# State's product in 32x32 tiles, the out product's last third moved by one step, y's squares summed head by head

## The reference

```
retention:  Q, K = xpos(xn W_Q), xpos(xn W_K)      8 heads of 32; K by the inverse scale
            V    = xn W_V
            Y_h  = (Q_h K_h^T * D_h) V_h           D_h[s,t] = gamma_h^(s-t) for s >= t, else 0
            Yn   = (Y - mean) / sqrt(var + 1e-5)   mean and variance over each head's 32 numbers
            out  = (silu(xn W_G) * (Yn * gn_weight + gn_bias)) W_O
feed-forward: xq = fp4(xn), weights in fp4 too     blocks of 16 along the last dimension
            h    = silu(xq Wgate^T) * (xq Wup^T)   704 wide
            out  = fp4(h) Wdown^T
```

## Time and profile before

| | us |
|---|---|
| median of 3 runs | 902.4 (901.42 to 902.75) |
| the profiled execution | 902.86 |
| its span in the trace | 901.1 |
| PE busy | 868.1 (96%) |
| DVE busy | 834.8 (93%) |
| POOL busy | 679.6 (75%) |
| ACT busy | 495.2 (55%) |

### The profile page before, as it was taken

One profiled execution on the slowest core, in us unless ns is written; L12 is line 12 of the kernel. 1 busy time (PEld: TensorE's weight loads), 2 busy tenths in 40 slices (PEclk: granted clock), 3 DMA queues, 4 the chain that ended last, 5 costly groups with the idle time before them and its releaser, 6 DMA issues.

```text
span 901.1 us, 20383 instructions
## 1 busy us (share of the span) xinstructions
PE 868.1 (96%) x7698; PEld 763.9 (85%) x7698; DVE 834.8 (93%) x1883; ACT 495.2 (55%) x1370; POOL 679.6 (75%) x795
## 2 busy tenths in 40 slices
PE   2889999999999999999999999999999999999996
PEld 1768888888888888888888888888888888888885
DVE  7879999999999999999999999999999999999984
ACT  5655555555555555555555555555555555555542
POOL 4767787777778777777877877787787777778774
PEclk9899999999999999999999999999999999999999
DMA  9200110110111011011101101100110110110000
GB/s 339 73 1 19 36 37 19 36 37 22 32 36 36 19 37 36 20 35 36 33 23 36 36 19 37 36 31 25 36 37 19 36 37 24 31 37 12 8 13 18
DMA packets 30049, 33.62 MB, mean 37 GB/s; under 512 B 3328, under 2 KB 28672, under 8 KB 29696
## 3 DMA queue, kind: packets, MB, share of 16 engines
q1 hardware_dynamic: 29808, 32.26, 11.4%
q10 hardware_dynamic: 144, 0.07, 0.0%
HBM read 23.92 MB, written 8.39 MB: 36 GB/s over the span
## 4 chain that ended last, share of the span: by engine, by line
PE 93%; POOL 3%; DVE 2%; ACT 1%; issue 1%; DMA 0%; POOLq 0%; DVEq 0%
PE quad L899 12%; PE quad L901 12%; PE quad L900 12%; PE quad L1080 5%; PE quad L961 4%; PE quad L984 4%; PE bank L901 3%; PE bank L900 3%; PE bank L899 3%; PE bank L1017 3%; PE quad L1087 3%; PE quad L926 3%; PE quad L1064 3%; PE quad L985 2%; PE quad L949 2%; PE quad L953 2%
## 5 line engine op out<-in xcount | busy, mean ns | idle before, releaser
L899 PE MATMUL quad<-w_gu_hi,xqT_hi 128*128 128x512 f32 (+1 forms) x384 | 150.3, 391 | 0.9 <-DVE xqT_lo L592 0.9
L901 PE MATMUL quad<-w_gu_hi,xqT_lo 128*128 128x512 f32 (+1 forms) x384 | 144.4, 376 | 0.0
L900 PE MATMUL quad<-w_gu_lo,xqT_hi 128*128 128x512 f32 (+1 forms) x384 | 143.3, 373 | 0.0
L463 POOL TENSOR_TENSOR rstd<-var_eps,power 128x9 f32<-128x9 f32 x67 | 124.1, 1853 | 5.6
L452 POOL TENSOR_TENSOR x_quot<-xn,x_inv 128x256 f32<-128x256 f32 x64 | 40.4, 632 | 90.9 <-DVE x_inv L640 90.9
L471 POOL TENSOR_TENSOR xT_lo<-xT_in,xT_hi 128x256 fp32r<-128x256 f32 x64 | 47.4, 740 | 61.7 <-ACT xT_hi L789 61.7
L438 POOL TENSOR_TENSOR h_quot<-h,h_inv 128x704 f32<-128x704 f32 x64 | 88.8, 1388 | 6.3 <-DVE h_inv L583 1.3
L721 ACT ACTIVATE xqT_hi<-bank 128x256 fp32r<-128x256 f32 x64 | 24.6, 384 | 121.1 <-PE bank L934 121.1
L448 POOL TENSOR_TENSOR qk<-qk_cos,qk_sin 128x512 f32<-128x512 f32 x64 | 82.8, 1293 | 7.6 <-PE bank L971 0.9
L487 POOL TENSOR_TENSOR gate_gn<-gate,gn 128x512 f32<-128x512 f32 x64 | 83.3, 1301 | 0.2 <-ACT gate L782 0.2
L901 PEld LDWEIGHTS quad<-w_gu_hi,xqT_lo 128*128 128x128 f32 x384 | 72.5, 189 | 11.5
(11 more groups left out here) (178 smaller groups left out, 2953.6 us busy)
## 6 DMA issues: line engine op xcount, KB each, us to landing
x_in<-in_x_dram SPq DMA_DIRECT2D x64, 128.0 KB, 2.1
xT_in<-in_xT_dram SPq DMA_DIRECT2D x64, 128.0 KB, 2.2
out_dram<-y_out SPq DMA_DIRECT2D x64, 128.0 KB, 1.7
sin<-const_sin_dram SPq DMA_DIRECT2D x1, 1792.0 KB, 10.9
raw<-in_w_gu_dram SPq DMA_DIRECT2D x2, 512.0 KB, 6.5
w_qkvg<-in_w_qkvg_dram SPq DMA_DIRECT2D x1, 1024.0 KB, 7.3
cos<-const_cos_dram SPq DMA_DIRECT2D x1, 896.0 KB, 7.0
raw<-in_w_down_dram SPq DMA_DIRECT2D x2, 352.0 KB, 7.7
```

What stands on the lines that cost most here:

```text
L463: pool.tensor_tensor(rstd[:, (t + 3) % RING, 0:1 + H], var_eps[:], power[:], ALU.pow).then_inc(rstd_ready, 1)
L899: pe.matmul(out, hi[:, k], w_hi[:, k], start=start, stop=False)
L900: pe.matmul(out, hi[:, k], w_lo[:, k], start=False, stop=False)
L901: return pe.matmul(out, lo[:, k], w_hi[:, k], start=False, stop=stop)
```

## The change

Three edits, made together. First, the state stays compact: `state` is the 128x64 sum itself, and its product is eight 32x32 matrix products with 128 moving columns, on eight different tiles of the array: for the first four heads rows r and columns r, for the last four rows r+1 and columns r. For this the last four heads of q and k are stored rotated by one (weights, cos and sin tables in the order `ORDER`), `probs` is read rotated (L961), and K^T V is written rotated (L971). ACT's four copies and POOL's clearing of `state` go. The product moves from ahead of x's transposes to between h's transposes and L961. Second, L1087 moves from the end of step i to behind the q and k product of step i+1, and DVE's y_out moves behind the first half of the masking. Third, ACT squares y with eight instructions of 32 columns, each of which also sums its columns into `moments` (`accum_out`); DVE's sum L648 goes, and POOL waits for ACT alone.

```diff
+ORDER = [*range(HG), *(HG + (r - 1) % HG for r in range(HG))]
-        for h in range(H):
+        for h in ORDER:
-        state_sum = sb("state_sum", [P, G * HD])
-        state = sb("state", [P, D])
+        state = sb("state", [P, G * HD])
+        def quarter(r):
+            return slice(r * HD, (r + 1) * HD)
+        def place(g, r):
+            return quarter((r + g) % HG)
 # POOL
-            pool.memset(state[:], 0.0).then_inc(cleared, 1)
-                        pool.wait_ge(y_var, t + 1)
+                        pool.wait_ge(squared, t + 1)
 # DVE: y_out (sum of b_out and x_in, L576) moves behind masked0 and h_inv
-                    dve.wait_ge(squared, t + 1)
-                    dve.tensor_reduce(moments[:, 2:], heads(y_sq[:]), AX_X, ALU.add).then_inc(y_var, 1)
+                    dve.wait_ge(kv_ready, kept_upto(t))
-                        dve.tensor_tensor(state_sum[:], state_sum[:], b_kv[:, 0:G * HD], ALU.add).then_inc(kv_add, 1)
+                        dve.tensor_tensor(state[:], state[:], b_kv[:, 0:G * HD], ALU.add).then_inc(kv_add, 1)
 # ACT
-                    act.activation(y_sq[:], b_y[:, 0:D], ACT.Square, scale=HD ** -0.5).then_inc(squared, 1)
+                    for head in range(H):
+                        dims = slice(head * HD, (head + 1) * HD)
+                        ins = act.activation(y_sq[:, dims], b_y[:, dims], ACT.Square, scale=HD ** -0.5, accum_out=moments[:, 2 + head:3 + head])
+                    ins.then_inc(squared, 1)
-                    act.wait_ge(kv_add, kept_upto(t))
-                    for r in range(HG):
-                        rows = slice(r * HD, (r + 1) * HD)
-                        ins = act.activation(tiles(state[:])[rows, :, rows], heads(state_sum[:])[rows], ACT.Copy)
-                    ins.then_inc(state_copy, 1)
 # PE, behind the q and k product
-                    pe.wait_ge(state_copy, kept_upto(t - 1))
-                    pe.wait_ge(masked1, t + 1)
-                    for g in range(G):
-                        ins = pe.matmul(b_yT[g], state[:, g * P:(g + 1) * P], qT[:, g, :], start=True, stop=False)
-                    ins.then_inc(st_ready, 1)
+                if exists(i - 3):
+                    t = i - 3
+                    for k in range(KD):
+                        ins = pe.matmul(b_out, zT_lo[:, k], w_out_hi[:, k], start=False, stop=k == KD - 1)
+                    ins.then_inc(out_ready, 1)
 # PE, behind the transposes of h
+                if exists(i - 1) and later(i - 1):
+                    t = i - 1
+                    for g in range(G):
+                        for r in range(HG):
+                            rows = place(g, r)
+                            ins = pe.matmul(b_yT[g][quarter(r), :], state[rows, g * HD:(g + 1) * HD], qT[rows, g, :], start=True, stop=False)
+                    ins.then_inc(st_ready, 1)
-                            ins = pe.matmul(b_yT[g][rows, :], val[:, head:head + HD], probs[:, r, g * P:(g + 1) * P],
+                            ins = pe.matmul(b_yT[g][quarter(r), :], val[:, head:head + HD], probs[:, (r + g) % HG, g * P:(g + 1) * P],
-                            ins = pe.matmul(b_kv[rows, g * HD:(g + 1) * HD], qk[:, D + head:D + head + HD], val[:, head:head + HD],
+                            key, head = D + g * P + place(g, r).start, (g * HG + r) * HD
+                            ins = pe.matmul(b_kv[place(g, r), g * HD:(g + 1) * HD], qk[:, key:key + HD], val[:, head:head + HD],
 # PE, at the end of the step
-                if exists(i - 2):
-                    t = i - 2
-                    for k in range(KD):
-                        ins = pe.matmul(b_out, zT_lo[:, k], w_out_hi[:, k], start=False, stop=k == KD - 1)
-                    ins.then_inc(out_ready, 1)
```

More of the change, by code:

```diff
@@ L223, in block_kernel @@
         x_peak = sem("x_peak")
-        summed = sem("summed")
         masked0 = sem("masked0")
         h_inverted = sem("h_inverted")
+        summed = sem("summed")
         rope_sin = sem("rope_sin")
@@ L238, in block_kernel @@
         x_inverted = sem("x_inverted")
-        y_var = sem("y_var")
         h_gridded = sem("h_gridded")
@@ L283, in block_kernel @@
         x_high = sem("x_high")
-        state_copy = sem("state_copy")
         x_normed = sem("x_normed")
         qk_ready = sem("qk_ready")
-        st_ready = sem("st_ready")
+        out_ready = sem("out_ready")
         x_turned = sem("x_turned")
@@ L293, in block_kernel @@
         h1_turned = sem("h1_turned")
+        st_ready = sem("st_ready")
         yT_ready = sem("yT_ready")
@@ L307, in block_kernel @@
         s_ready = sem("s_ready")
-        out_ready = sem("out_ready")
         def exists(t):
@@ L424, in _ @@
             pool.memset(moments[:], 1.0).then_inc(cleared, 1)
-            pool.memset(state[:], 0.0).then_inc(cleared, 1)
-            pool.wait_ge(cleared, 3)
+            pool.wait_ge(cleared, 2)
             def step(i):
@@ L570, in step @@
                     dve.tensor_reduce(x_max[:], blocks(xn[:, t % 2, :]), AX_X, ALU.max, apply_absolute_value=True).then_inc(x_peak, 1)
[L571 to L576, removed]
                 if exists(i - 1):
@@ L583, in step @@
                     dve.tensor_scalar(h_inv[:], h_rec[:], SIX, 1e12, ALU.mult, ALU.min).then_inc(h_inverted, 1)
+                if exists(i - 3):
+                    t = i - 3
+                    dve.wait_ge(out_ready, t + 1)
+                    if t >= 2:
+                        dve.wait_ge(stored, 16 * (t - 1))
+                    dve.tensor_tensor(y_out[:, t % 2, :], b_out, x_in[:, t % SLOTS, :], ALU.add).then_inc(summed, 1)
                 if exists(i):
@@ L617, in step @@
                     if t == 0:
-                        dve.wait_ge(cleared, 3)
+                        dve.wait_ge(cleared, 2)
                     dve.wait_ge(x_stats, t + 1)
@@ L666, in step @@
                     t = i - 1
+                    dve.wait_ge(kv_ready, kept_upto(t))
                     if t % CHUNKS == 0:
-                        dve.tensor_copy(state_sum[:], b_kv[:, 0:G * HD]).then_inc(kv_add, 1)
+                        dve.tensor_copy(state[:], b_kv[:, 0:G * HD]).then_inc(kv_add, 1)
                     else:
-                        dve.tensor_tensor(state_sum[:], state_sum[:], b_kv[:, 0:G * HD], ALU.add).then_inc(kv_add, 1)
+                        dve.tensor_tensor(state[:], state[:], b_kv[:, 0:G * HD], ALU.add).then_inc(kv_add, 1)
                 if exists(i):
@@ L876, in load_functions @@
             def load_functions():
-                act.wait_ge(cleared, 3)
+                act.wait_ge(cleared, 2)
                 act.activation(scratch[:], power[:], ACT.Silu)
@@ L920, in step @@
                         turn_rest(8)
-                if exists(i - 1) and later(i - 1):
-                    t = i - 1
-                    pe.wait_ge(state_copy, kept_upto(t - 1))
-                    pe.wait_ge(masked1, t + 1)
-                    for g in range(G):
-                        ins = pe.matmul(b_yT[g], state[:, g * P:(g + 1) * P], qT[:, g, :], start=True, stop=False)
-                    ins.then_inc(st_ready, 1)
+                if exists(i - 3):
+                    t = i - 3
+                    for k in range(KD):
+                        ins = pe.matmul(b_out, zT_lo[:, k], w_out_hi[:, k], start=False, stop=k == KD - 1)
+                    ins.then_inc(out_ready, 1)
                 if exists(i):
@@ L959, in step @@
                         for r in range(HG):
-                            rows, head = slice(r * HD, (r + 1) * HD), (g * HG + r) * HD
-                            ins = pe.matmul(b_yT[g][rows, :], val[:, head:head + HD], probs[:, r, g * P:(g + 1) * P],
+                            head = (g * HG + r) * HD
+                            ins = pe.matmul(b_yT[g][quarter(r), :], val[:, head:head + HD], probs[:, (r + g) % HG, g * P:(g + 1) * P],
                                             start=t % CHUNKS == 0, stop=True)
@@ L1193, in layouts @@
     heads = lambda w: w.transpose(0, 2, 1).reshape(D, D)
+    w_q, w_k = w_q[ORDER], w_k[ORDER]
     w_gu = [w[c * GW:min((c + 1) * GW, F)] for c in (2, 1, 0) for w in (w_gate, w_up)]
```

5 lines of the change are left out of this document (removed).

## The result

The changed kernel takes 906.44 us (median of 6 runs, 904.88 to 907.48) against 901.91 us (6 runs, 901.34 to 903.11) for the kernel before on the same chip: ratio 1.0044, 95% interval 1.0034 to 1.0054. It is slower by 0.44%; forecast was 902.2, no change. The profiled execution took 906.24 with a span of 904.4, that is 3.4 and 3.3 more than before.

What follows compares the result with a forecast made beforehand. PE was taken as the bound, with z on POOL limiting savings ahead of its transposes. From 902.86 us, -0.7 for the steps and +0.5 for the ends gave 902.7 profiled, 902.2 median; range 896 to 917.

Steps and rivals of the forecast that it cites:

- the size of the state's product in 32x32 tiles: PE, behind z's transposes: sixteen 32x32 instructions, eight tiles at once, taken as 0.33 us per step.
- the extra: PE, between the state's product and L961: 0.09 us more for changing form from 32x32 to 128x32.
- the second weight load: PE, L1087 behind the 32-row scores: 0.11 us per step lost, expected to go once q and k follow the scores.
- the cap: PE ahead of z's transposes: waiting for POOL's z limits the saving to 0.35 of 0.55 us per step.
- Rival D: PE at z's transposes: no wait for z, the full 0.55 us is had, -13.2 us, 889.5; chance 0.05.
- Rival B: PE, state's product: four passes at a time whatever the tiles, 0.44 or 0.57 us, 908.5 or 915.8; chance 0.30.
- Rival A: PE, state's product: eight at once, no extra between small forms, 0.23 us, 896.7 in all; chance 0.15.
- the squares: ACT, y's squares: eight pairs take 1.7 us, 0.21 each; x_magic waits, z isn't later.
- the ends: Start and end of the kernel, where POOL waits for the moments: longer squares show there, +0.5 us in all.
- C: ACT, y's squares: a pair every 0.35 us makes z 0.7 late in each of 64 steps, about 947; chance 0.12.
- the forecast's own mechanism: PE per step: -0.35 ahead of z's transposes, +0.33 for the product behind them; chance 0.35, own range 900 to 905.

Runs made afterwards that it cites:

- l1087_only: The kernel before with only L1087 and y_out moved: 904.57 us, ratio 1.0024 to the kernel before.
- diag_zfirst: Changed kernel with POOL's z issued ahead of gate_gn, both head groups on the same four 32x32 tiles: 910.55 us (one run), 12.9 over that kernel with eight tiles.
- nosq_zfirst: Changed kernel without the squares edit, with POOL's z issued ahead of gate_gn: 897.59 us, ratio 0.9944 to the kernel before.

## Why the prediction was wrong, point by point

*Failed: the size of the state's product in 32x32 tiles.* "I take 0.33: eight tiles at once, with the extra." It is 0.378. Eight at once was right (sixteen starts in two groups; 0.218 for the streams), and so was the extra of 0.09 for one more change of form (0.088). What the term had at 0.02 (0.33 less 0.22 and 0.09) is the time that small tiles take to get going, which is 0.07: 0.024 for the first group and 0.047 for eight starts one after the other. The first part stood in the rows, where L961 takes 0.46 and not the 16 x 0.11 / 4 = 0.44 of the text; the second no row of before shows for eight tiles. The change from full to small tiles is paid as before, in h's transposes (0.748 with any small tiles behind them, 0.655 with the full product). 56 x 0.048 = 2.7 of the 3.5 us by which the profiled execution (906.24) stands above the 902.7 forecast for it.

*Wrong, but without effect on the sum: what is lost behind the scores.* "I read it as the second weight load, which is not hidden behind so short a matmul." With 512 columns the same tenth is lost at once, and the records of the weight loads point to the first load rather than the second (l1087_only, not isolated). No tenth went, so 0.447 and not 0.55 was taken away ahead of z's transposes. The cap at z hid the error: the wait is 0.107 where 0.20 to 0.25 was forecast, and the gain is the same.

*Right: the cap.* "0.35 per step is all that a saving on PE ahead of z's transposes can give"; measured 0.335 (3.269 to 2.934 from the scores to the end of z's transposes). z keeps 4.71, its transposes start 0.05 behind it. Rival D is out: without z's wait the step is 13.173, 0.06 less than before, and D's 0.22 was too much as well, since 0.447 and not 0.55 is taken away. Rival B's pace is out for eight tiles and true for four: diag_zfirst has 0.569, the 0.57 that B gave. Rival A is out: the change of form is paid, and the start of the groups too.

*Right in the end, wrong on the way: the squares.* Eight pairs take 1.5 (one every 0.17, forecast 0.21). x_magic was forecast to wait for them; it waits for x_quot, which takes 1233 ns instead of 632. The two groups on the page of the kernel before were these.
```profile
L452 POOL TENSOR_TENSOR x_quot<-xn,x_inv 128x256 f32<-128x256 f32 x64 | 40.4, 632 | 90.9 <-DVE x_inv L640 90.9
...
L650 DVE SCALAR_TENSOR_TENSOR h_grid<-h_magic,h_diff 128x704 f16<-128x704 bf16 x64 | 76.5, 1196 | 0.0
```
There x_quot started 0.16 ahead of h_grid (timelines of POOL and of DVE before):
```profile
453.84 0.62 POOL L452 TENSOR_TENSOR x_quot<-xn,x_inv 128x256 f32<-128x256 f32 x1 [1.50 <-DVE x_inv L640]
```
```profile
454.00 1.21 DVE L650 SCALAR_TENSOR_TENSOR h_grid<-h_magic,h_diff 128x704 f16<-128x704 bf16 x1
```
Freed of the sum by head, DVE starts h_grid first, 0.13 ahead of x_quot (timelines of DVE and of POOL after):
```profile
454.55 0.89 DVE L655 SCALAR_TENSOR_TENSOR h_grid<-h_magic,h_diff 128x704 f16<-128x704 bf16 x1
```
```profile
454.68 1.24 POOL L459 TENSOR_TENSOR x_quot<-xn,x_inv 128x256 f32<-128x256 f32 x1 [1.36 <-DVE x_inv L647]
455.90 0.26 POOL L468 TENSOR_SCALAR var_eps<-moments 128x9 f32<-128x9 f32 x1
```
h_grid takes 892 ns instead of 1196, x_quot ends 0.48 behind it, and var_eps, which used to lie beside h_grid, falls from 910 to 260 ns. The squares alone bring this about, and without them it is gone (nosq_zfirst). The Trainium skill ("SBUF — State Buffer", SBUF: two separate sides) says that whichever starts first, a DVE instruction with two SBUF inputs or one of GpSimd that reads SBUF, holds the shared ports for its whole length and blocks the other. The trace agrees in both orders on which of the two gets longer, though by less than they overlap: h_grid by 0.30 of 0.46 before, x_quot by 0.60 of 0.76 after. The prediction did not weigh it. var_eps ends no later than before, so rstd, y_gain and z are not delayed, and it costs nothing.

*Wrong, small: the ends.* +0.5 was forecast for start and end, 0.2 is seen, within what they vary by; 0.015 per step at the down product and behind it (0.8 us in all) was not forecast and is unexplained.

*Chances.* Slower had 0.47, all but 0.05 of it on rivals B and C. It became slower by the forecast's own mechanism with one term 0.05 too small. A sum of -0.01 that stands on a term known only between 0.22 and 0.57 can't carry "no change" as the forecast; the prediction's own chances had slower (0.47) ahead of the same (0.25).

## What to carry to other kernels

Before work is moved, ask which side of the next wait it stands on: the product was taken from a place where only 0.335 of its 0.447 counted and put where each nanosecond does. The remedy was not on the bound engine but one instruction swapped on POOL, and only together with the change (0.9995 alone, 1.0044 the change, 0.9955 both). Small tiles pay by the number of different tiles in flight, less a price each time the form changes and another for starting the tiles one by one, so a piece of only two groups gains little: here it takes 0.378, of which 0.218 are streams, against 0.447 with full tiles.

## What the runs showed of the hardware that was not expected

- 32x32 passes of 128 columns: eight on eight tiles in 0.109, four on four tiles in 0.11. The first group takes 0.133, and neighbouring starts lie 0.007 apart (0.047 for eight). A change from 32x32 to 128x32 tiles costs 0.088, about the 0.093 from full to small.
- The first full matmul behind 32-row ones takes 0.107 longer, with 256 or 512 columns alike; its weight load starts with it and not ahead of it.
- An ACT squaring of 32 columns with its read of the accumulator comes every 0.17, although the two records last 0.21 and 0.22: they overlap.
- A POOL instruction beside a DVE one with two SBUF inputs: 632 or 1233 ns (x_quot), 260 or 910 ns (var_eps), by which of the two starts first.
